# First two attention units of a cross-attention and mixture-of-experts kernel: clears first on GpSimd, the second unit's norms beside the first's, loads in another order

## The chip, the core and the metric

The kernel runs on one core of one Trainium2 chip. The metric is the device time in microseconds (us). The engines are named as in the profile: PE is TensorE (matmuls and transposes) and PEld its weight loads, DVE is VectorE, ACT is ScalarE, POOL is GpSimd, and SP is SyncE, which here only starts DMAs.

## The reference, cut to what matters

```python
def xattn(q, k, v):                      # 8 heads, along the sequence axis of 512
    qn, kn = _l2norm(qh), _l2norm(kh)    # x / max(sqrt(sum(x*x)), 1e-12), 64 values each
    qk = 5.0 * einsum('bhdq,bhdk->bhqk', qn, kn)
    return einsum('bhqk,bhdk->bhdq', softmax(qk), vh)
x = x + xattn(_layernorm(x), ctx_2048, ctx_2048)
x = x + ffn(_layernorm(x))               # 4 experts, top 2 of 4, capacity 512, d 512, hidden 2048
```

x and the context are (4, 512, 512) in float32. The change touches only the first layer norm and the two l2 norms of the attention, of its first two units.

## The kernel before

A unit of attention is 128 rows of x, that is two heads of one batch; there are 16, written as (batch, 0 or 1). For each unit the engines do this:

- DVE takes mean and variance of the x rows (`statistics`, L775 to L781), POOL raises the variance to the power -0.5 (`prepare`, L476, result `rstd`), and DVE writes `x_norm` (`normalize`, L787).
- PE transposes `x_norm` through `bank_m` (`transpose_queries`, L1238) and the context rows through `bank_t` (`values`, L1245). ACT squares both (L617, L625), DVE sums the squares (L794, L804) and floors them (`ss_max`, L797, L807), POOL raises them to -0.5 (`query_norms`, `key_norms`, L476, result `rnorm`).
- DVE widens the queries' factors to 512 columns (`widen_queries`, L836, `wide_q`), PE transposes them back into `bank_m` (`spread_queries`, L1253), and DVE forms the scaled queries as a rounded part and a remainder (`queries`: `q_f` L822, `q_hi` L824, `q_lo` L830).
- ACT rounds the keys (`round_keys`, L642, `k_hi`), POOL takes their remainders (`key_remainders`, L500, `k_lo`). PE then multiplies three terms for the scores (L1266), ACT takes the exponentials (L652), PE the weighted values (L1276) and the sums (L1288).

The order on each engine is written out by hand. `unit(u, behind, ahead)` on each engine works on unit u and on parts of the units beside it: PE begins it with the values and the spread of the next unit, and in its middle transposes the queries of the unit after that. What stands ahead of the first `unit` is a prologue, and the change lies there. In it `bank_m` serves the transposes and the spread of unit (0,0), and then the transposes of (0,1), which wait for `q_hi` of (0,0); `x_norm` is one buffer. POOL also clears `x_got` and `o_got` (L519, L526), 128x2048 each, which are not read before the experts. `cst` is one tile of constants: its first 128 columns are the identity for the transposes, and they come by one DMA (L389), the other 709 columns by a second (L390).

After the attention come the router's choice and then the experts' two matrix products. They are the same in both kernels.

Of the kernel before, what the change touches and what calls it, by code (L numbers as in the profile page):

```python
# [15 lines left out]
ALU = mybir.AluOpType  # L16
ACT = mybir.ActivationFunctionType
# [76 lines left out]
def xattn_moe_kernel(nc, x, ctx_in, Wg, bg, W1, W2, consts, out):  # L94
# [6 lines left out]
    with ExitStack() as stack:  # L101
# [68 lines left out]
        with ExitStack() as phase:  # L170
            def att(name, shape, dt=F32):
                return phase.enter_context(nc.sbuf_tensor(name, shape, dt))
# [3 lines left out]
            c_sq = att("c_sq", [P, D])  # L176
            x_norm = att("x_norm", [P, D])
            x_sq = att("x_sq", [P, D])
# [190 lines left out]
        def _(sp):  # L369
# [16 lines left out]

            load_x((0, 0))
            load_c((0, 0))
            sp.dma_start(ident, consts[:, C_IDENT:C_IDENT + P]).then_inc(ident_in, 16)  # L389
            sp.dma_start(cst[:, C_BEFORE:], consts[:, C_BEFORE:]).then_inc(cst_in, 16)  # L390
            sp.dma_start(wg[:, :, :], Wg.rearrange("(k p) e -> p k e", p=P)).then_inc(wg_in, 16)
            load_x((0, 1))
            load_c((0, 1))
            sp.dma_start(bgb[:, :], bg.rearrange("(a e) -> a e", a=1).broadcast_to([P, E])).then_inc(bg_in, 16)
# [79 lines left out]
        def _(pool):  # L474
# [37 lines left out]
            def finish(u):  # L512
                n = number(u)
                pool.wait_ge(var2_done, n + 1)
                inv_sqrt(rstd2[u[1]][:, :], var2_e[u[1]][:, :], 1).then_inc(rstd2_done, 1)

            prepare((0, 0))
            prepare((0, 1))
            nc.gpsimd.memset(x_got[:, :, :], 0.0).then_inc(got_clear, 1)  # L519
            query_norms((0, 0))  # L520
            key_remainders((0, 0))
            key_norms((0, 0))
            key_remainders((0, 1))
            query_norms((0, 1))
            prepare((1, 0))
            nc.gpsimd.memset(o_got[:, :, :], 0.0).then_inc(got_clear, 1)  # L526

# [82 lines left out]
        def _(act):  # L610
            def square_queries(u, reused):

                n = number(u)
                act.wait_ge(xt_done, n + 1)
                if reused:
                    act.wait_ge(ssq_done, n)
                nc.scalar.activation(x_sq[:, :], bank_m[:, :], ACT.Square).then_inc(xsq_done, 1)  # L617

# [72 lines left out]
            take_v((0, 0), 0)  # L691
            square_queries((0, 1), True)
            round_keys((0, 1), False)
# [76 lines left out]
        def _(dve):  # L770
# [12 lines left out]
            def normalize(u):  # L783

                n = number(u)
                dve.wait_ge(rstd_done, n + 1)
                nc.vector.tensor_scalar(x_norm[:, :], x_all[:, bass.ds(n, 1), :].rearrange("p a d -> p (a d)"),  # L787
                                        mv[u[1]][:, 0:1], rstd[u[1]][:, 0:1], ALU.subtract, ALU.mult).then_inc(xn_done, 1)
# [28 lines left out]
            def queries(u, follow):  # L817


                n = number(u)  # L820
                dve.wait_ge(rq_ready, n + 1)
                nc.vector.scalar_tensor_tensor(q_f[:, :], x_norm[:, :], ALPHA, bank_m[:, :], ALU.mult, ALU.mult  # L822
                                               ).then_inc(q_done, 1)
                nc.vector.scalar_tensor_tensor(q_hi[u[1]][:, :], x_norm[:, :], ALPHA, bank_m[:, :],  # L824
                                               ALU.mult, ALU.mult).then_inc(qhi_done, 1)
                dve.wait_ge(q_done, n + 1)
                dve.wait_ge(qhi_done, n + 1)
                if follow is not None:
                    normalize(follow)
                nc.vector.tensor_tensor(q_lo[u[1]][:, :], q_f[:, :], q_hi[u[1]][:, :].bitcast(F32), ALU.subtract  # L830
                                        ).then_inc(q_split, 1)
# [64 lines left out]
            statistics((0, 1))  # L896
            sum_query_squares((0, 0))
            widen_queries((0, 0))
            sum_key_squares((0, 0))
            queries((0, 0), None)  # L900
            normalize((0, 1))
            dve.wait_ge(cst_in, 16)
# [4 lines left out]
            for n in range(2):  # L907
                nc.vector.tensor_copy(parts[:, :, :, n], cst[:, C_TOK + n * UNITS:C_TOK + (n + 1) * UNITS]
                                      .unsqueeze(1).broadcast_to([P, E, UNITS])).then_inc(bf_done, 1)
            sum_query_squares((0, 1))  # L910
            statistics((1, 0))
            widen_queries((0, 1))

# [319 lines left out]
        def _(pe):  # L1233
            def transpose_queries(u):

                pe.wait_ge(xn_done, number(u) + 1)
                for t in range(TT):
                    last = nc.tensor.transpose(bank_m[:, t * P:(t + 1) * P], x_norm[:, t * P:(t + 1) * P], ident)  # L1238
                last.then_inc(xt_done, 1)
# [68 lines left out]
            pe.wait_ge(ident_in, 16)  # L1308
            pe.wait_ge(cst_in, 16)
            transpose_queries((0, 0))  # L1310
            values((0, 0))
            spread_queries((0, 0))
            pe.wait_ge(qhi_done, 1)
            transpose_queries((0, 1))
            pe.wait_ge(q_split, 1)
            pe.wait_ge(k_split, 1)
            scores((0, 0), 0, False)
            scores((0, 0), 1, False)

            def unit(u, behind, ahead):  # L1320
# [184 lines left out]
```

## Time and profile before

| | us |
|---|---|
| median of 3 runs | 631.37 (631.08 to 632.15) |
| the profiled execution, its own time | 629.77 |
| its span, first to last instruction | 628.0 |
| PE busy | 567.1 (90%) |
| DVE busy | 357.0 (57%) |
| ACT busy | 281.6 (45%) |
| POOL busy | 186.2 (30%) |

A timeline's row gives the start in the span, the busy time, the engine, the line, the operation, the tiles (output<-inputs), the shape and how many instructions are merged, and in brackets how long the engine had been idle and what ended that. Rows of PE overlap, since matmuls are pipelined. A released engine's start is the time at which its last input was there, plus a tenth of a microsecond or so.

### The profile page before, as it was taken

The page shows a single profiled execution, that of the slowest core. Times are in us where ns is not written, and L with a number is a line of the kernel's source. Part 1 is how long each engine was busy: PE and PEld are TensorE (multiplying, and loading weights), DVE is VectorE, ACT ScalarE, POOL GpSimd, SP SyncE. Part 2 cuts the span into 40 slices and gives each one's busy share as a digit, 9 for nine tenths or more (in the row PEclk, how much of TensorE's full clock was granted, in tenths as well). Part 3 has the DMA queues.
Part 4 walks back from the last instruction along what each step waited for, and adds up shares of the span by engine and source line. Part 5 has one row for each costly group of instructions (what it writes and reads, how often), then busy time and mean ns, then how long its engine had stood idle before and what let it go on. Part 6 is the DMA issues. An engine that isn't in the chain of part 4 may idle for free.

```text
span 628.0 us, 8727 instructions
## 1 busy us (share of the span) xinstructions
PE 567.1 (90%) x2842; PEld 407.4 (65%) x2842; DVE 357.0 (57%) x702; ACT 281.6 (45%) x421; POOL 186.2 (30%) x143
## 2 busy tenths in 40 slices
PE   1799999999999512999999999999999999999994
PEld 1445455455454401688888888888888788888883
DVE  4879899899988784534336443354543444424212
ACT  2587776776777240433243333433434324333320
POOL 4556656656642342200030330210420400500002
PEclk9999999999999755699999999999999999999998
DMA  5422332333312113332341543333452332442001
GB/s 144 159 96 85 118 132 89 117 123 95 102 69 94 75 67 103 99 134 68 134 134 68 183 151 134 100 100 110 157 179 88 117 120 97 172 163 68 0 1 67
DMA packets 46600, 67.73 MB, mean 108 GB/s; under 512 B 8560, under 2 KB 25072, under 8 KB 46576
## 3 DMA queue, kind: packets, MB, share of 16 engines
q1 hardware_dynamic: 42736, 54.84, 26.0%
q0 software_dynamic: 3840, 12.59, 6.0%
q8 instruction: 13, 0.21, 0.1%
q14 instruction: 11, 0.09, 0.1%
HBM read 54.70 MB, written 12.64 MB: 107 GB/s over the span
## 4 chain that ended last, share of the span: by engine, by line
PE 64%; DVE 5%; issue 4%; POOL 1%; DMA 1%; POOLq 0%; DVEq 0%; ACT 0%; SPq 0%
PE two L1423 29%; PE four L1453 9%; PE four L1452 9%; PE four L1450 9%; PE two L1276 2%; PE four L1266 2%; DVE junk L1045 1%; PE two L1288 1%; PE bank_t L1304 1%; DMA x_got<-x2n_dram,idx_all 1%; POOL w_lo L532 1%; DMA p_inv<-inv_dram 0%; PE bank_t L1411 0%; PE bank_m L1411 0%; DVE onehot L1132 0%
## 5 line engine op out<-in xcount | busy, mean ns | idle before, releaser
L758 ACT ACTIVATE h_f<-two 128x512 f32<-128x512 f32 x64 | 38.3, 599 | 231.4 <-PE two L1423 231.4
L1206 DVE TENSOR_TENSOR h_lo<-h_f,h_hi 128x512 fp32r<-128x512 f32 x64 | 44.1, 690 | 125.9 <-ACT h_hi L759 125.9
L1423 PE MATMUL two<-xt_hi,w_hi 128*128 (+1 forms) x256 | 102.9, 402 | 0.7 <-ACT xt_hi L747 0.7
L1423 PE MATMUL two<-xt_hi,w_lo 128*128 (+1 forms) x256 | 101.3, 396 | 0.0
L1423 PE MATMUL two<-xt_lo,w_hi 128*128 (+1 forms) x256 | 100.7, 396 | 0.0
L1453 PE MATMUL four<-w_hi,h_lo 128*128 128x512 f32 x256 | 100.5, 393 | 0.0
L1450 PE MATMUL four<-w_hi,h_hi 128*128 128x512 f32 x256 | 100.5, 392 | 0.0
L1452 PE MATMUL four<-w_lo,h_hi 128*128 128x512 f32 x256 | 100.4, 392 | 0.0
L652 ACT ACTIVATE prob<-four,rnorm 128x512 f32<-128x512 f32 x128 | 77.6, 688 | 25.3 <-POOL rnorm L476 18.2
L1176 DVE TENSOR_TENSOR w_lo<-raw,w_hi 128x2048 fp32r<-128x2048 f32 x30 | 68.7, 2291 | 23.3 <-ACT w_hi L685 23.3
L476 POOL TENSOR_TENSOR rnorm<-ss_max,power 128x8 f32<-128x8 f32 x32 | 64.6, 2018 | 49.6 <-DVE ss_max L807 48.3
L605 POOL DMA_INDIRECT out<-o_got,idx_all x16 | 20.2, 1264 | 165.4 <-DVE o_got L1227 163.0
L584 POOL DMA_INDIRECT x_got<-x2n_dram,idx_all x16 | 23.9, 1496 | 140.0 <-DVE idx_all L1163 125.3
L1276 PE MATMUL two<-prob,v_t 128*64 128x512 f32 x256 | 62.0, 605 | 0.0
L685 ACT ACTIVATE w_hi<-raw 128x2048 fp32r<-128x2048 f32 x32 | 61.3, 1918 | 0.0
L1423 PEld LDWEIGHTS two<-xt_hi,w_hi 128*128 128x128 f32 x256 | 48.6, 190 | 11.7 <-ACT xt_hi L747 1.1
L1423 PEld LDWEIGHTS two<-xt_hi,w_lo 128*128 128x128 f32 x256 | 48.6, 190 | 11.1
L1423 PEld LDWEIGHTS two<-xt_lo,w_hi 128*128 128x128 f32 x256 | 48.7, 190 | 10.7
L1453 PEld LDWEIGHTS four<-w_hi,h_lo 128*128 128x128 f32 x256 | 48.1, 188 | 10.8
L1450 PEld LDWEIGHTS four<-w_hi,h_hi 128*128 128x128 f32 x256 | 48.1, 188 | 10.8
L1452 PEld LDWEIGHTS four<-w_lo,h_hi 128*128 128x128 f32 x256 | 48.1, 188 | 10.7
L855 DVE TENSOR_TENSOR half_sum<-prob 128x512 f32<-128x512 f32 x64 | 41.5, 690 | 0.1
(174 smaller groups left out, 741.3 us busy)
## 6 DMA issues: line engine op xcount, KB each, us to landing
raw<-in_L_ffn_W SPq DMA_DIRECT2D x64, 512.0 KB, 4.0
x_all<-in_x SPq DMA_DIRECT2D x16, 256.0 KB, 2.7
c_sb<-in_ctx SPq DMA_DIRECT2D x16, 256.0 KB, 2.8
out<-x_all SPq DMA_DIRECT2D x16, 256.0 KB, 2.0
x2n_dram<-x2n SPq DMA_DIRECT2D x16, 256.0 KB, 2.0
p_inv<-inv_dram SPq DMA_DIRECT2D x30, 128.0 KB, 2.8
few<-p_sum SPq DMA_DIRECT2D x30, 2.0 KB, 2.2
cst<-in_consts SPq DMA_DIRECT2D x1, 354.5 KB, 4.2
```

Of the source, the lines that this page charges most:

```text
L476: return nc.gpsimd.tensor_tensor(dst, src, power[:, 0:n], ALU.pow)
L652: last = nc.scalar.activation(prob[h][t][:, :], s_ps[:, 2 * (t % 2) + h, :], ACT.Exp, scale=rnorm[u[1]][:, 0, t, h:h + 1])
L685: nc.scalar.activation(w_hi[c % SPLIT_BUFS][:, :], raw[c % RAW_BUFS][:, :], ACT.Copy).then_inc(whi_done, 1)
L758: nc.scalar.activation(h_f[m % 2][:, :], z_ps[m % 2][:, :], ACT.Gelu)
L855: nc.vector.tensor_tensor(half_sum[h][n][:, :], prob[h][2 * n][:, :], prob[h][2 * n + 1][:, :], ALU.add).then_inc(halves_done[h], 1)
L1176: nc.vector.tensor_tensor(w_lo[c % SPLIT_BUFS][:, :], raw[c % RAW_BUFS][:, :], w_hi[c % SPLIT_BUFS][:, :].bitcast(F32), ALU.subtract).then ...
L1206: nc.vector.tensor_tensor(h_lo[m % 2][:, :], h_f[m % 2][:, :], h_hi[m % 2][:, :].bitcast(F32), ALU.subtract).then_inc(h_split, 1)
L1276: last = nc.tensor.matmul(o_ps[0][DH * h:DH * (h + 1), :], v_t[u[1]][:, t, h, :], prob[h][t][:, :], start=(t == 0), stop=(t == TT - 1))
L1423: return nc.tensor.matmul(z[:, :], w_part[c][:, w], x_k, start=start, stop=stop)
L1450: nc.tensor.matmul(acc_ps[:, t, :], h_hi[m % 2][:, h], w_hi[c][:, w], start=(m == 0), stop=False)
L1452: nc.tensor.matmul(acc_ps[:, t, :], h_hi[m % 2][:, h], w_lo[c][:, w], start=False, stop=False)
L1453: last = nc.tensor.matmul(acc_ps[:, t, :], h_lo[m % 2][:, h], w_hi[c][:, w], start=False, stop=(m == MT - 1))
```

## The change

SP loads in another order: x of (0,0), the identity, the context of (0,0), x and context of (0,1), and then the other constants and the router's weights. POOL makes both clears at its very start, takes the keys' remainders of (0,0) before the second unit's `rstd` (with a wait for `x_norm`), and raises the query norms of (0,1) ahead of the keys' remainders of (0,1). `x_norm` has two buffers. On PE the transposes of (0,1) go into `two[0]`, which is also `o_ps[0]`, and stand ahead of the spread of (0,0); the wait for the other constants stands behind the first scores. ACT squares the queries of (0,1) from there. DVE normalizes (0,1) and sums its query squares between the steps of (0,0).

```diff
-            x_norm = att("x_norm", [P, D])
+            x_norm = [att(f"x_norm{n}", [P, D]) for n in range(2)]
...
             load_x((0, 0))
+            sp.dma_start(ident, consts[:, C_IDENT:C_IDENT + P]).then_inc(ident_in, 16)
             load_c((0, 0))
-            sp.dma_start(ident, consts[:, C_IDENT:C_IDENT + P]).then_inc(ident_in, 16)
+            load_x((0, 1))
+            load_c((0, 1))
             sp.dma_start(cst[:, C_BEFORE:], consts[:, C_BEFORE:]).then_inc(cst_in, 16)
             sp.dma_start(wg[:, :, :], Wg.rearrange("(k p) e -> p k e", p=P)).then_inc(wg_in, 16)
-            load_x((0, 1))
-            load_c((0, 1))
...
+            nc.gpsimd.memset(x_got[:, :, :], 0.0).then_inc(got_clear, 1)
+            nc.gpsimd.memset(o_got[:, :, :], 0.0).then_inc(got_clear, 1)
             prepare((0, 0))
+            pool.wait_ge(xn_done, 1)
+            key_remainders((0, 0))
             prepare((0, 1))
-            nc.gpsimd.memset(x_got[:, :, :], 0.0).then_inc(got_clear, 1)
             query_norms((0, 0))
-            key_remainders((0, 0))
             key_norms((0, 0))
+            query_norms((0, 1))
             key_remainders((0, 1))
-            query_norms((0, 1))
             prepare((1, 0))
-            nc.gpsimd.memset(o_got[:, :, :], 0.0).then_inc(got_clear, 1)
...
-            square_queries((0, 1), True)
+            square_queries((0, 1), True, o_ps[0])
...
             sum_query_squares((0, 0))
+            normalize((0, 1))
+            sum_key_squares((0, 0))
             widen_queries((0, 0))
-            sum_key_squares((0, 0))
+            sum_query_squares((0, 1))
             queries((0, 0), None)
-            normalize((0, 1))
+            widen_queries((0, 1))
...
-            sum_query_squares((0, 1))
             statistics((1, 0))
-            widen_queries((0, 1))
...
             pe.wait_ge(ident_in, 16)
-            pe.wait_ge(cst_in, 16)
             transpose_queries((0, 0))
             values((0, 0))
+            transpose_queries((0, 1), o_ps[0])
             spread_queries((0, 0))
-            pe.wait_ge(qhi_done, 1)
-            transpose_queries((0, 1))
             pe.wait_ge(q_split, 1)
             pe.wait_ge(k_split, 1)
             scores((0, 0), 0, False)
             scores((0, 0), 1, False)
+            pe.wait_ge(cst_in, 16)
```

POOL, from the start of the program to the remainders of the second unit's keys; `rstd` and `rnorm` carry the number of the unit. Before:

```order
L478 MEMSET power 128x16
L476 ISA
L476 TENSOR_TENSOR rstd0<-var_e0,power 128x1
L476 TENSOR_TENSOR rstd1<-var_e1,power 128x1
L519 MEMSET x_got 128x2048
L476 TENSOR_TENSOR rnorm0<-ss_max,power 128x8
L500 TENSOR_TENSOR k_lo0<-c_sb0,k_hi0 128x512
L476 TENSOR_TENSOR rnorm0<-ss_max,power 128x8
L500 TENSOR_TENSOR k_lo1<-c_sb1,k_hi1 128x512
```

And now:

```order
L478 MEMSET power 128x16
L517 MEMSET x_got 128x2048
L518 MEMSET o_got 128x2048
L476 ISA
L476 TENSOR_TENSOR rstd0<-var_e0,power 128x1
L500 TENSOR_TENSOR k_lo0<-c_sb0,k_hi0 128x512
L476 TENSOR_TENSOR rstd1<-var_e1,power 128x1
L476 TENSOR_TENSOR rnorm0<-ss_max,power 128x8 x2
L476 TENSOR_TENSOR rnorm1<-ss_max,power 128x8
L500 TENSOR_TENSOR k_lo1<-c_sb1,k_hi1 128x512
```

Between the floors and the powers of the first unit's query norms no clear and no remainder stands any more; the ISA row, a reload of the library of instructions that the power comes from, has moved behind the two clears.

DVE, from the sum of the first unit's query squares to its `q_lo`. Before:

```order
L794 TENSOR_REDUCE ss<-x_sq 128x8
L797 TENSOR_SCALAR ss_max<-ss 128x8
L836 COPY wide_q<-rnorm0 128x512
L804 TENSOR_REDUCE ss<-c_sq 128x8
L807 TENSOR_SCALAR ss_max<-ss 128x8
L822 SCALAR_TENSOR_TENSOR q_f<-x_norm,bank_m 128x512
L824 SCALAR_TENSOR_TENSOR q_hi0<-x_norm,bank_m 128x512
L830 TENSOR_TENSOR q_lo0<-q_f,q_hi0 128x512
L787 TENSOR_SCALAR x_norm<-x_all,mv1,rstd1 128x512
```

And now:

```order
L795 TENSOR_REDUCE ss<-x_sq 128x8
L798 TENSOR_SCALAR ss_max<-ss 128x8
L788 TENSOR_SCALAR x_norm1<-x_all,mv1,rstd1 128x512
L805 TENSOR_REDUCE ss<-c_sq 128x8
L808 TENSOR_SCALAR ss_max<-ss 128x8
L837 COPY wide_q<-rnorm0 128x512
L795 TENSOR_REDUCE ss<-x_sq 128x8
L798 TENSOR_SCALAR ss_max<-ss 128x8
L823 SCALAR_TENSOR_TENSOR q_f<-x_norm0,bank_m 128x512
L825 SCALAR_TENSOR_TENSOR q_hi0<-x_norm0,bank_m 128x512
L831 TENSOR_TENSOR q_lo0<-q_f,q_hi0 128x512
L837 COPY wide_q<-rnorm1 128x512
```

The second unit's `x_norm` and query sums have come ahead of the first unit's queries, and its `wide_q` right behind them.

PE, from its first transposes to the first scores. Before:

```order
L1238 MATMUL bank_m<-cst,x_norm 128x128 x4
L1245 MATMUL bank_t<-cst,c_sb0 128x128 x4
L1253 MATMUL bank_m<-cst,wide_q 128x128 x4
L1238 MATMUL bank_m<-cst,x_norm 128x128 x4
L1266 MATMUL four<-q_hi0,k_hi0 128x512 x2
```

And now:

```order
L1239 MATMUL bank_m<-cst,x_norm0 128x128 x4
L1246 MATMUL bank_t<-cst,c_sb0 128x128 x4
L1239 MATMUL two0<-cst,x_norm1 128x128 x4
L1254 MATMUL bank_m<-cst,wide_q 128x128 x4
L1267 MATMUL four<-q_hi0,k_hi0 128x512 x2
```

The second unit's transposes no longer stand between the first unit's spread and its scores.

## Rows read from the trace of the kernel before

**Rows 1.** The page: PE and its granted clock in 40 equal slices.

```profile
PE   1799999999999512999999999999999999999994
PEclk9999999999999755699999999999999999999998
```

**Rows 2.** Busy time in one stretch: length, PE, PEld, DVE, ACT, POOL, granted clock, DMA.

```profile
33.59:43.83 10.24, 10.24 (x63) 4.94 (x61) 7.95 (x19) 8.12 (x14) 5.92 (x5) 1.00 0.19 59
```

**Rows 3.** Timeline of PE, the first 34 us.

```profile
6.45 1.09 PE L1238 MATMUL bank_m<-cst,x_norm 128*128 128x128 f32 x4 [6.45 <-DMA cst<-in_consts]
7.33 1.06 PE L1245 MATMUL bank_t<-cst,c_sb 128*128 128x128 f32 x4
14.03 1.11 PE L1253 MATMUL bank_m<-cst,wide_q 128*128 128x128 f32 x4 [5.64 <-DVE wide_q L836]
17.87 1.09 PE L1238 MATMUL bank_m<-cst,x_norm 128*128 128x128 f32 x4 [2.73 <-DVE x_norm L787]
18.89 0.80 PE L1266 MATMUL four<-q_hi,k_hi 64*128 64x512 f32 x2
...
21.75 0.74 PE L1245 MATMUL bank_t<-cst,c_sb 128*128 128x128 f32 x4
23.80 0.66 PE L1253 MATMUL bank_m<-cst,wide_q 128*128 128x128 f32 x4 [1.31 <-DVE wide_q L836]
...
28.42 0.50 PE L1266 MATMUL four<-q_hi,k_hi 64*128 64x512 f32 x2
```

**Rows 4.** Timeline of DVE, the first 30 us.

```profile
4.41 0.15 DVE L781 TENSOR_SCALAR var_e<-mv 128x1 f32<-128x1 f32 x1
5.33 0.55 DVE L787 TENSOR_SCALAR x_norm<-x_all,mv,rstd 128x512 f32<-128x512 f32 x1 [0.76 <-POOL rstd L476]
7.21 0.69 DVE L775 BATCH_NORM_STATS2 stats<-x_all 128x6 f32<-128x512 f32 x1 [1.34 <-DMA x_all<-in_x]
...
8.23 0.68 DVE L794 TENSOR_REDUCE ss<-x_sq 128x8 f32<-128x512 f32 x1
8.94 1.79 DVE L797 TENSOR_SCALAR ss_max<-ss 128x8 f32<-128x8 f32 x1
12.49 1.48 DVE L836 COPY wide_q<-rnorm 128x512 f32<-128x512 f32 x1 [1.76 <-POOL rnorm L476]
...
14.60 0.17 DVE L807 TENSOR_SCALAR ss_max<-ss 128x8 f32<-128x8 f32 x1
15.18 0.69 DVE L822 SCALAR_TENSOR_TENSOR q_f<-x_norm,bank_m 128x512 f32<-128x512 f32 x1 [0.41 <-PE bank_m L1253]
...
16.58 0.69 DVE L830 TENSOR_TENSOR q_lo<-q_f,q_hi 128x512 fp32r<-128x512 f32 x1
...
23.31 0.43 DVE L836 COPY wide_q<-rnorm 128x512 f32<-128x512 f32 x1 [0.81 <-POOL rnorm L476]
...
26.50 0.69 DVE L830 TENSOR_TENSOR q_lo<-q_f,q_hi 128x512 fp32r<-128x512 f32 x1
```

**Rows 5.** Timeline of POOL, the first 30 us.

```profile
4.72 0.57 POOL L476 TENSOR_TENSOR rstd<-var_e,power 128x1 f32<-128x1 f32 x1 [3.88 <-DVE var_e L781]
...
8.91 1.80 POOL L519 MEMSET x_got<- 128x2048 f32 x1
10.81 1.65 POOL L476 TENSOR_TENSOR rnorm<-ss_max,power 128x8 f32<-128x8 f32 x1
12.43 1.26 POOL L500 TENSOR_TENSOR k_lo<-c_sb,k_hi 128x512 fp32r<-128x512 f32 x1
...
28.07 4.08 POOL L476 TENSOR_TENSOR rnorm<-ss_max,power 128x8 f32<-128x8 f32 x2 [2.51 <-DVE ss_max L807]
```

**Rows 6.** Timeline of SP's queue: the start of the second unit's load of x.

```profile
3.08 0.51 SPq L372 DMA_DIRECT2D x_all<-in_x  x1
```

**Rows 7.** One tile's instructions: shortest, median and longest in ns.

```profile
L855 DVE TENSOR_TENSOR half_sum<-prob x64: 636/691/694, 27.9 to 199.8; 128x512 f32<-128x512 f32 x64
```

**Rows 8.** Busy time in a stretch at the experts' start, columns as in rows 2.

```profile
260.00:265.00 5.00, 5.00 (x21) 4.03 (x20) 1.48 (x2) 3.71 (x5) 0.00 (x0) 0.91 0.02 5
```

More of the change, by code:

```diff
@@ L610, in _, with square_queries @@
         def _(act):
-            def square_queries(u, reused):
+            def square_queries(u, reused, bank=bank_m):
                 n = number(u)
@@ L616, in square_queries @@
                     act.wait_ge(ssq_done, n)
-                nc.scalar.activation(x_sq[:, :], bank_m[:, :], ACT.Square).then_inc(xsq_done, 1)
+                nc.scalar.activation(x_sq[:, :], bank[:, :], ACT.Square).then_inc(xsq_done, 1)
             def square_keys(u, behind):
@@ L786, in normalize @@
                 dve.wait_ge(rstd_done, n + 1)
-                nc.vector.tensor_scalar(x_norm[:, :], x_all[:, bass.ds(n, 1), :].rearrange("p a d -> p (a d)"),
+                nc.vector.tensor_scalar(x_norm[u[1]][:, :], x_all[:, bass.ds(n, 1), :].rearrange("p a d -> p (a d)"),
                                         mv[u[1]][:, 0:1], rstd[u[1]][:, 0:1], ALU.subtract, ALU.mult).then_inc(xn_done, 1)
@@ L821, in queries @@
                 dve.wait_ge(rq_ready, n + 1)
-                nc.vector.scalar_tensor_tensor(q_f[:, :], x_norm[:, :], ALPHA, bank_m[:, :], ALU.mult, ALU.mult
+                nc.vector.scalar_tensor_tensor(q_f[:, :], x_norm[u[1]][:, :], ALPHA, bank_m[:, :], ALU.mult, ALU.mult
                                                ).then_inc(q_done, 1)
-                nc.vector.scalar_tensor_tensor(q_hi[u[1]][:, :], x_norm[:, :], ALPHA, bank_m[:, :],
+                nc.vector.scalar_tensor_tensor(q_hi[u[1]][:, :], x_norm[u[1]][:, :], ALPHA, bank_m[:, :],
                                                ALU.mult, ALU.mult).then_inc(qhi_done, 1)
@@ L1233, in _, with transpose_queries @@
         def _(pe):
-            def transpose_queries(u):
+            def transpose_queries(u, bank=bank_m):
                 pe.wait_ge(xn_done, number(u) + 1)
                 for t in range(TT):
-                    last = nc.tensor.transpose(bank_m[:, t * P:(t + 1) * P], x_norm[:, t * P:(t + 1) * P], ident)
+                    last = nc.tensor.transpose(bank[:, t * P:(t + 1) * P], x_norm[u[1]][:, t * P:(t + 1) * P], ident)
                 last.then_inc(xt_done, 1)
```

## The prediction, as it was made before the changed kernel ran

> **What bounds the kernel now.** I read the page's slices first [rows 1]. PE is busy at nine tenths or more in all but the first slice, slices 14 to 16, and the last, so the end is set by PE's work plus the stretches in which PE has none. One of these is the start: 15.7 us pass before the first slice is over. A stretch of the second unit [rows 2] shows PE busy for 10.24 of 10.24 us while DVE has 7.95, ACT 8.12 and POOL 5.92. From the first unit on, then, the attention runs at PE's pace, and whatever brings PE's first full unit forward brings all that follows forward by as much. The stages behind work on data, not on a clock of their own, and their loads are started by semaphores of the same units. Next I read the timeline of PE [rows 3]: up to 18.89, where the first scores begin, it does 16 transposes in 18.89 us, with idle gaps of 6.45, 5.64 and 2.73 us, and a fourth of 1.31 us at 23.80, behind which there are no more. So the number to follow is the start of the second unit's spread, 23.80. The timelines of DVE and POOL [rows 4, 5] say what each gap waits for.
>
> **The first transposes.** They begin at 6.45, released by the other constants, though `x_norm` is done at 5.33 + 0.55 = 5.88 [rows 3, 4]. The transposes read the identity alone. With the wait moved and the identity second in the queue, they begin 0.06 us behind `x_norm`, as the spread did behind `wide_q` (12.49 + 1.48 = 13.97 to 14.03), so at 5.94: 0.51 us earlier. The clears must be over by then. Each is 1.80 us [rows 5]; from about 0.9 the two end at 4.5, and `rstd` is wanted at 4.72. That covers them by 0.2 us, if the ISA row behind them is short; I take nothing for it, and its upper end is a rival below. The second unit's x, issued as sixth at 3.08 and used at 7.21 [rows 4, 6], is now fourth; with some 830 KB ahead of and in it instead of 1.2 MB I estimate 5.4 from these times, ahead of 5.88, where DVE comes to it. Its statistics were over about 1.0 us behind their start (7.21 to the next sum at 8.23), so now at about 7.0, ahead of the sum of the squares. The first keys' context comes 0.3 us later and is wanted by ACT only for `k_hi`, which POOL needs at 5.9.
>
> **The floor and the clear.** The sum of query squares begins 1.78 us behind the first transposes (8.23 - 6.45), so at 7.72, and `ss_max` 0.71 us later at 8.43. It took 1.79 us before, and the same operation on the keys 0.17 [rows 4]; the long one ended with POOL's clear of `x_got` (8.94 + 1.79 = 10.73 and 8.91 + 1.80 = 10.71) [rows 5]. With no clear there it takes 0.17: 1.62 us saved. It ends at 8.60, and the power runs 8.68 to 10.33 (1.65) [rows 5].
>
> **The widening and the remainders.** `wide_q` took 1.48 us at 12.49 and 0.43 at 23.31; the first lay beside `k_lo` (12.43 + 1.26) [rows 4, 5]. Now `k_lo` runs behind `x_norm` at 5.9 to 7.2, and `rstd` of (0,1) behind it, 7.3 to 7.8, wanted at 8.6. So `wide_q` takes 0.43: 1.05 us saved. The Trainium skill, Advanced Engine Details and Errata, VectorE Performance Modes, says why: the second Vector port is shared, and two-port Vector instructions and GpSimd's block each other. The trace agrees with its 1.79 and 1.48.
> Together 0.51 + 1.62 + 1.05 = 3.18: the first spread moves from 14.03 to 10.85. What is put ahead of it on PE, the transposes of (0,1), needs `x_norm1`, which DVE writes at 8.6 to 9.2; they run 9.3 to 10.4 and are over. On DVE the normalizing (0.55) and the keys' sum and floor (0.68 + 0.17) fill 8.6 to 10.1, under the power's 10.33. Behind the spread DVE sums the second query squares at about 11.0 to 11.9, and the spread's result is there at 10.85 + 1.11 = 11.96. All that costs nothing, though the last by 0.1 us only.
>
> **The first queries and scores.** `q_f` to the end of `q_lo` is 15.18 to 17.27, 2.09 us; now 12.00 to 14.09. Before, the transposes of (0,1) came between `q_lo` and the scores at 18.89; with them gone the scores begin about 0.1 us behind `q_lo`, at 14.2. That is 4.7 us earlier, of which 1.5 is this step.
>
> **The second unit's spread.** The first scores took 21.75 - 18.89 = 2.86 us, then the values; so the values start at 17.06 and the spread could follow. It waited 1.31 us for `wide_q` of (0,1). Now POOL has that unit's factors by about 13.7 (10.33 + 1.65 for the keys' power, then 1.65), takes `k_lo1` to 15.1, and DVE copies by 15.8, all ahead of 17.9. But PE's clock: four transposes took 1.09 to 1.11 us at 6.45, 14.03 and 17.87, 0.74 at 21.75 and 0.66 at 23.80, while the granted clock stands at full there [rows 1]. PE had then worked without a gap for 3.9 us, from 17.87. I put the rise as long behind 14.2, near 18.1, so the values and a part of the spread still run at the lower level of 1.2 GHz: the values take their 0.88 (7.33 - 6.45), and the spread starts at 17.94, 5.86 us earlier; half the spread and the first scores behind it lose 0.35. **Sum: 5.5 us.** The next queries have slack: `q_lo` of (0,1) ended at 26.50 + 0.69 = 27.19, its scores began at 28.42 by PE's order, 1.2 us of cover for DVE's constants' casts and the two statistics, which now stand ahead of them.
>
> **Bounds.** The clock: if it were already up for the first scores, these would gain another 1.2 us; if it rose 2.5 us later, 1.1 would go. It falls and rises once more around the router's choice (slices 14 to 18, and 0.91 in a stretch at the experts' start [rows 8]), and where in the work it rises can move by some 1 us either way. `q_lo1`'s neighbour: `k_lo1` on POOL starts near 13.7, while DVE is at `q_lo` of (0,0), which reads two SBUF tiles. No row shows that pair. The nearest are `half_sum`, which also reads two tiles and kept its 691 ns (636 to 694) [rows 7] beside powers that themselves took 2.04 instead of 1.65 (4.08 for two) [rows 5], and `wide_q`, which was held for all of `k_lo`. So 0 to 1.1 us; I take 0, as `q_lo` is the kind of `half_sum`.
>
> **Rivals.** (A) The ISA row, a reload of a library. Before, it lay in the 3.88 us in which POOL idled ahead of `rstd`, so its cost is between 0 and 3.9, and nothing shows it. Behind the clears at 4.5 it would put `rstd` at up to 8.4 instead of 4.72: 3.7 us of the 5.5 lost, 1.8 left, 629.5. For it: a wait of unknown content. Against: no DMA but the kernel's own is at work in these microseconds.
> The Trainium skill, GPSIMD Engine Reference, Instruction dispatch, says that the first call behind a load of a library pays about 6 us. By that figure the gain would be gone (4.5 + 6 = 10.5, 0.3 slower than now); the 3.88 of the trace leaves no room for it.
> (B) The port between `q_lo` and `k_lo1`, and behind it a late `wide_q` and late statistics: 1.1 us at the scores, and up to 1 more at the second queries, beyond their 1.2 of cover; 3.4 to 4.4 left, 627.5.
> (C) Slower: PE's clock. Its gaps are spread differently, and the rise may come much later than 3.9 us behind 14.2. A microsecond of PE's work at the lower level loses 1 - 0.66/1.10 = 0.4 us. To be 1.3 us slower than before it must cost 6.8 us, so the rise has to come some 17 us late, past 35. It decides from there; 632.7. Against: it has come after 3.9 us of unbroken work, and from 14.2 the work is unbroken.
> (D) The shift does not reach the end, as another engine or a wait further on sets the end of the attention: no change, 631.4. Against: [rows 2].
>
> **How the numbers follow.** The span is 628.0, the execution 629.77 with it, the median of the runs 631.37, 1.6 above. The gain is the same for all: 628.0 - 5.5 = 622.5 for the span, 624.3 for the execution, 625.9 for the median. Forecast 0.73, from 624.2 to 627.0; A 0.09, 626.4 to 629.5; B 0.09, 627.0 to 628.0; C 0.04; D 0.05. The range 624.2 to 628.2 takes in all of B and half of A and leaves out under 2 in 10, the forecast's own tails among them. A measurement of this kernel can tell about 0.2%, 1.3 us, from no change: faster 0.90, same 0.06, slower 0.04.
>
> **What would show it.** In the profile of the changed kernel: first transposes at 5.9, `ss_max` and `wide_q` of (0,0) at 0.17 and 0.43 us, the first scores at 14.2, no idle time of PE between them and the third unit, the second spread near 18.0, and each later unit 5.5 us earlier. `rstd` later than 4.8 is A; `q_lo` longer than 0.75 us or PE idle between the second spread and the second scores is B; transposes of 1.1 us behind 21 is C. I am wrong if these starts are met and the span has not moved with them.

## The result

| | before | changed |
|---|---|---|
| median of 5 runs each | 631.37 us | 624.11 us (622.89 to 624.97) |
| ratio, 95% interval | | 0.9892 (0.9876 to 0.9907) |
| the profiled execution | 629.77 us | 624.58 us |
| its span | 628.0 us | 622.8 us |

The kernel is faster by 1.1%, by 6.8 us if the ratio is put on 631.37 (5.9 to 7.8). The forecast had 5.5. The span it gave, 622.5, was met within 0.3 us. The median it gave, 625.9, is 1.8 too high: 624.11 lies 0.1 below the low end of the range, and 631.37 times the ratio, 624.55, lies 0.35 inside it. Why the span fits and the median doesn't is the main question of the experiments. One execution of one experiment's kernel, 842 us at a granted clock of 0.65, is in none of the numbers below.

The page of the changed kernel, PE and its granted clock in 40 slices, to be held against [rows 1]:

```profile
PE   3999999999998512999999999999999999999994
PEclk9999999999999655799999999999999999999998
```

The first two slices have changed, 3 and 9 tenths instead of 1 and 7. The thirteenth, 8 instead of 9, now ends inside the hole at the router, since the attention is over earlier. The rest is as before. The middle of the attention is too: a stretch of the second unit (length, PE, PEld, DVE, ACT, POOL, granted clock, DMA) shows PE full and the others with the room of [rows 2], and `half_sum` keeps its 0.69 us [rows 7].

```profile
28.68:38.92 10.24, 10.24 (x62) 4.92 (x60) 7.93 (x19) 8.12 (x14) 5.41 (x5) 1.00 0.24 57
L856 DVE TENSOR_TENSOR half_sum<-prob x64: 634/690/694, 22.5 to 195.1; 128x512 f32<-128x512 f32 x64
```

The timeline of PE, for [rows 3]:

```profile
5.97 1.09 PE L1239 MATMUL bank_m<-cst,x_norm 128*128 128x128 f32 x4 [5.97 <-DVE x_norm L788]
9.12 1.11 PE L1239 MATMUL two<-cst,x_norm 128*128 128x128 f32 x4 [1.21 <-DVE x_norm L788]
11.08 1.12 PE L1254 MATMUL bank_m<-cst,wide_q 128*128 128x128 f32 x4 [0.85 <-DVE wide_q L837]
14.38 0.79 PE L1267 MATMUL four<-q_hi,k_hi 64*128 64x512 f32 x2 [2.18 <-DVE q_lo L831]
...
18.15 1.06 PE L1254 MATMUL bank_m<-cst,wide_q 128*128 128x128 f32 x4
19.14 0.80 PE L1267 MATMUL four<-q_hi,k_hi 64*128 64x512 f32 x2
19.73 0.47 PE L1267 MATMUL four<-q_lo,k_hi 64*128 64x512 f32 x2
...
29.18 0.60 PE L1254 MATMUL bank_m<-cst,wide_q 128*128 128x128 f32 x4
```

and the spread of the third unit in the kernel before, which ends the prologue there:

```profile
34.09 0.60 PE L1253 MATMUL bank_m<-cst,wide_q 128*128 128x128 f32 x4
```

PE's four gaps before were 6.45, 5.64, 2.73 and 1.31 us, 16.13 in all. Now there are four others, 5.97, 1.21, 0.85 and 2.18, 10.21 in all, and behind 14.38 PE has none. The second spread comes 23.80 - 18.15 = 5.65 us earlier, the third 34.09 - 29.18 = 4.91, since PE did its first full unit more slowly than before: the pair of score matmuls still takes 0.80 us at 19.14, and 0.47 at 19.73 is the first faster one. From the third spread on the lead hardly moves. It is 4.9 at the first transposes of `key_w` in the router (207.52 to 202.62), 5.0 at the last of them (221.40 to 216.36) and at the experts' start (255.97 to 251.01) and 5.2 at the end of the span.

Timelines of DVE and then POOL, for [rows 4, 5]:

```profile
5.28 0.55 DVE L788 TENSOR_SCALAR x_norm<-x_all,mv,rstd 128x512 f32<-128x512 f32 x1 [0.69 <-POOL rstd L476]
6.41 0.69 DVE L776 BATCH_NORM_STATS2 stats<-x_all 128x6 f32<-128x512 f32 x1 [0.58 <-DMA x_all<-in_x]
...
8.44 0.17 DVE L798 TENSOR_SCALAR ss_max<-ss 128x8 f32<-128x8 f32 x1
...
10.60 0.43 DVE L837 COPY wide_q<-rnorm 128x512 f32<-128x512 f32 x1 [0.74 <-POOL rnorm L476]
...
13.63 0.69 DVE L831 TENSOR_TENSOR q_lo<-q_f,q_hi 128x512 fp32r<-128x512 f32 x1
14.24 1.50 DVE L837 COPY wide_q<-rnorm 128x512 f32<-128x512 f32 x1
```

```profile
2.64 1.80 POOL L518 MEMSET o_got<- 128x2048 f32 x1
4.67 0.57 POOL L476 TENSOR_TENSOR rstd<-var_e,power 128x1 f32<-128x1 f32 x1 [0.22 <-DVE var_e L782]
6.50 1.27 POOL L500 TENSOR_TENSOR k_lo<-c_sb,k_hi 128x512 fp32r<-128x512 f32 x1 [1.26 <-ACT k_hi L643]
...
8.69 5.09 POOL L476 TENSOR_TENSOR rnorm<-ss_max,power 128x8 f32<-128x8 f32 x3 [0.28 <-DVE ss_max L798]
13.76 1.70 POOL L500 TENSOR_TENSOR k_lo<-c_sb,k_hi 128x512 fp32r<-128x512 f32 x1
```

### The profile page after: what moved, and what is told of

It reads as the page before. It is cut to its first block, busy times and chain, and to the rows that moved or that the text cites. A ratio compares the mean times of both kernels' runs of the same rounds, so it can differ in the third digit from the quotient of the medians.

```text
span 622.8 us, 8726 instructions
## 1 busy us (share of the span) xinstructions
PE 568.2 (91%) x2842; PEld 408.5 (66%) x2842; DVE 354.3 (57%) x702; ACT 281.6 (45%) x421; POOL 187.0 (30%) x143
## 4 chain that ended last, share of the span: by engine, by line
PE 65%; DVE 5%; issue 4%; DMA 1%; POOL 1%; POOLq 0%; DVEq 0%; ACT 0%; SPq 0%
PE two L1423 29%; PE four L1453 9%; PE four L1452 9%; PE four L1450 9%; PE two L1277 2%; PE four L1267 2%; DVE junk L1046 1%; PE two L1289 1%; PE bank_t L1305 1%; DMA x_got<-x2n_dram,idx_all 1%; POOL w_lo L533 1%; DMA p_inv<-inv_dram 0%; PE bank_t L1411 0%; PE bank_m L1411 0%; DVE onehot L1133 0%
```

## The experiments

Lines of the changed kernel are one above those of before. No kernel here leaves out any of the computation. In each, "the third spread" is the start on PE of the third unit's spread, 34.09 in the kernel before. Up to it the prologue shows. Behind it each unit of the attention takes 10.2 to 12.0 us, and each takes the same in all traces to 0.04 us, but for three units with a wait for a load, which come up below.

### Before, twice more, and the changed kernel once more

No edit. They ask how typical the two profiled executions are.

> The kernel before itself, for a second trace of it. Its profiled span was 628.0 us, while its other runs have spans of 626.9 to 630.5 us, and the changed kernel's of 621.1 to 623.2, some 6.5 to 7 us less; the two traces show 4.9 us from the third unit to the router, and 5.2 at the end. If runs differ only in when PE's clock rises and falls and in loads landing a little later, a typical trace of before shows the missing 1.5 us in the prologue (third spread later than 34.1) or at the router and the experts' start. If it lies evenly in the attention's units, my account of a pure shift is wrong. Against itself the ratio is 1.000 within 0.2%.

> The kernel before itself for a third trace, if it can be had of a run with a span near its median (628.4 us on this chip). The shift seen between the traces is 4.9 us (first pair) and 5.9 us (second pair) at the third unit, and 5.2 and 5.4 at the end; the medians are 6.8 us apart. A typical trace shows where a further 1 us lies: in the prologue, at the router, or at the experts. Against itself 1.000.

> The changed kernel itself, on the chip of the kernels beside it, to have its distribution of spans next to theirs. The chain gives 4.9 us from the third unit on. If the fall of the median by 7.3 us in the first comparison was more than that (a real cost of the clears or loads later on), the ratio is again 0.989 and the spans differ by about 7 us; if it was the spread of runs, the ratio is 0.991 to 0.992 and the spans differ by 5 us.

Before against itself gave the ratios 0.9998 (0.9984 to 1.0012) and 0.9993 (0.9978 to 1.0008); the changed kernel again 0.9884 (0.9862 to 0.9907), median 623.57. Beside the experiments the kernel before ran 63 times, with a median of 630.4 and spans of 626.9 to 630.5, median 628.6. The changed kernel's nine spans are 621.1 to 623.2, median 621.9 (621.75 for the last four). The medians of the spans are thus 6.7 us apart. DVE's statistics of the second unit, in the kernel before the first and the second time more:

```profile
7.73 0.69 DVE L775 BATCH_NORM_STATS2 stats<-x_all 128x6 f32<-128x512 f32 x1 [1.76 <-DMA x_all<-in_x]
```

```profile
7.89 0.69 DVE L775 BATCH_NORM_STATS2 stats<-x_all 128x6 f32<-128x512 f32 x1 [2.10 <-DMA x_all<-in_x]
```

the third spread in the first of them:

```profile
34.61 0.60 PE L1253 MATMUL bank_m<-cst,wide_q 128*128 128x128 f32 x4
```

and PE in the second, then in the changed kernel again:

```profile
14.71 1.12 PE L1253 MATMUL bank_m<-cst,wide_q 128*128 128x128 f32 x4 [6.27 <-DVE wide_q L836]
...
34.75 0.60 PE L1253 MATMUL bank_m<-cst,wide_q 128*128 128x128 f32 x4
```

```profile
14.24 0.80 PE L1267 MATMUL four<-q_hi,k_hi 64*128 64x512 f32 x2 [2.18 <-DVE q_lo L831]
...
18.96 0.50 PE L1267 MATMUL four<-q_hi,k_hi 64*128 64x512 f32 x2
...
28.68 0.60 PE L1254 MATMUL bank_m<-cst,wide_q 128*128 128x128 f32 x4
```

In the trace that the prediction read, the second unit's x was there at 7.21; in the two others 0.52 and 0.68 us later, and the first spread stands later by as much, at 14.55 and 14.71 instead of 14.03. In the second of them the DMA sets the prologue, because the sum of the first unit's squares queues on DVE behind the second unit's statistics: it begins 2.41 us behind the first transposes instead of 1.78. (In the first of them the constants were 0.52 us late as well.) In the changed kernel x lands at 6.41 and 6.09, ahead of where it is missed. Its second trace also has the third spread 0.5 us earlier, 0.14 of it from the start of the scores and the rest from the clock, which was up at 18.96 instead of about 19.8.

So the lead at the third spread depends on the pair of traces: 4.9 in the first pair, 5.9 and 6.1 for the two others of before against the changed kernel again. But it isn't the whole of the scatter. The trace with 34.61, 0.5 later than 34.09, has the shorter span, 627.3 instead of 628.0. From the experts' first transposes to the last matmul it took 368.2 us and the other 368.9, and over all fourteen traces of this document this stage, whose instructions are the same everywhere, takes 368.0 to 369.6. With three traces of before (middle third spread 34.61) and two of the changed kernel (mean 28.93) the lead is 5.7 us of the 6.7. The last 1.0 us isn't traced to a place: single traces differ by more than that behind the router.

### The clears alone

```diff
+            nc.gpsimd.memset(x_got[:, :, :], 0.0).then_inc(got_clear, 1)
+            nc.gpsimd.memset(o_got[:, :, :], 0.0).then_inc(got_clear, 1)
             prepare((0, 0))
             prepare((0, 1))
-            nc.gpsimd.memset(x_got[:, :, :], 0.0).then_inc(got_clear, 1)
...
             prepare((1, 0))
-            nc.gpsimd.memset(o_got[:, :, :], 0.0).then_inc(got_clear, 1)
```

> The kernel before with one part of the change alone: both clears at POOL's start. My theory, the chain of the prologue: the first floor takes 0.17 us instead of 1.79, everything behind it moves by 1.6 us, the first remainders still lie beside the first wide_q (1.48 us), first scores at 17.3 instead of 18.9, gain 1.6 us (629.8 where before is 631.4). Rival, that the clear of o_got beside the first full unit also cost time, since the median fell by 2 us more than the span of the profiled execution did: gain above 2.5 us.

Ratio 0.998 (0.9964 to 0.9995), that is 1.3 us, and by the medians of the spans, 626.8 beside 628.5, 1.7. The 1.6 expected lies between, and the rival's 2.5 is out. DVE and PE in this kernel:

```profile
9.16 0.17 DVE L797 TENSOR_SCALAR ss_max<-ss 128x8 f32<-128x8 f32 x1
...
11.09 1.48 DVE L836 COPY wide_q<-rnorm 128x512 f32<-128x512 f32 x1 [1.76 <-POOL rnorm L476]
```

```profile
17.48 0.80 PE L1266 MATMUL four<-q_hi,k_hi 64*128 64x512 f32 x2
```

The floor takes 0.17 instead of 1.79, and `wide_q`, whose neighbour `k_lo` has stayed, its old 1.48. The chain from the floor to the scores holds. The third spread is at 32.68.

### The clears put back

The same two lines moved back to their old places in the changed kernel.

> The changed kernel with the two clears in their old places. Chain theory: the first floor takes 1.8 us again, first scores at 16.0 instead of 14.4, 1.6 us later. Since moving the first remainders back moved the first scores by 1.17 us and the third unit by 0.39 us only, PE's clock having risen at the same 19.5 us, I expect the third unit 0.6 to 1.6 us later, 1.1 us slower than the changed kernel. Rival, that the clears have no part in the result once the rest is in: 0.

Ratio 0.9899 (0.9876 to 0.9921), median 624.43 beside 623.57 of the changed kernel; the intervals overlap, so the trace has to tell. DVE, then PE:

```profile
8.52 1.63 DVE L798 TENSOR_SCALAR ss_max<-ss 128x8 f32<-128x8 f32 x1
```

```profile
15.72 0.80 PE L1267 MATMUL four<-q_hi,k_hi 64*128 64x512 f32 x2 [2.18 <-DVE q_lo L831]
...
19.07 0.60 PE L1254 MATMUL bank_m<-cst,wide_q 128*128 128x128 f32 x4
```

The floor is held again, and the scores come 1.34 us later than at 14.38, where 1.6 were expected. But PE is fast at 18.58 already, where the changed kernel was slow until 19.7, and the third spread, at 29.31, is only 0.1 us later (0.6 against the second trace; 0.6 to 1.6 were expected). In this trace the clock gives back most of what the clear takes.

### The first remainders put back

POOL in the changed kernel, in the old order again:

```diff
             prepare((0, 0))
-            pool.wait_ge(xn_done, 1)
-            key_remainders((0, 0))
             prepare((0, 1))
             query_norms((0, 0))
+            key_remainders((0, 0))
```

> The changed kernel with the first keys' remainders back between the two first norms on POOL. Chain theory with the shared port: the first wide_q takes 1.5 us again instead of 0.43, first scores at 15.4 instead of 14.4, 1.0 us slower than the changed kernel. Rival, that it is covered by the slack elsewhere: 0.

Ratio 0.9912 (0.9882 to 0.9943), median 624.97. `wide_q` and the scores:

```profile
10.72 1.49 DVE L836 COPY wide_q<-rnorm 128x512 f32<-128x512 f32 x1 [0.74 <-POOL rnorm L476]
```

```profile
15.55 0.79 PE L1266 MATMUL four<-q_hi,k_hi 64*128 64x512 f32 x2 [2.18 <-DVE q_lo L830]
```

`wide_q` is held for 1.49 us beside `k_lo`, and the scores come 1.17 later. The third spread is at 29.57, 0.4 later than in the changed kernel and 0.9 later than in its second trace. The mechanism is as told; its worth, as with the clears, depends on when the clock rises. The interval overlaps that of the changed kernel, so the 1.0 us expected is neither shown nor ruled out in the time.

### The second unit put back behind the first

PE, DVE and ACT of the changed kernel take the second unit's query steps in the old order:

```diff
-            transpose_queries((0, 1), o_ps[0])
             spread_queries((0, 0))
+            pe.wait_ge(qhi_done, 1)
+            transpose_queries((0, 1))
...
-            normalize((0, 1))
-            sum_key_squares((0, 0))
             widen_queries((0, 0))
-            sum_query_squares((0, 1))
+            sum_key_squares((0, 0))
             queries((0, 0), None)
-            widen_queries((0, 1))
+            normalize((0, 1))
...
+            sum_query_squares((0, 1))
             statistics((1, 0))
+            widen_queries((0, 1))
```

> The changed kernel with one part undone: the second unit's normalizing, transposes, squares and sums stand behind the first unit's queries again, in bank_m (two buffers of x_norm stay). Chain theory: the first spread stays at 11.1, the first scores wait for the four transposes (1.5 us, so 15.9), and the second spread again waits 1.3 us for its factors; second spread at 20.8 instead of 18.15, but then with PE's clock already up, so 2.0 us slower than the changed kernel, 3.0 us faster than before. Rival, that this part only shifts waits about: within 0.7 us of the changed kernel.

Ratio 0.9948 (0.993 to 0.9966), median of the spans 625.3. PE:

```profile
14.54 1.09 PE L1239 MATMUL bank_m<-cst,x_norm 128*128 128x128 f32 x4 [2.73 <-DVE x_norm L788]
...
20.48 0.66 PE L1254 MATMUL bank_m<-cst,wide_q 128*128 128x128 f32 x4 [1.35 <-DVE wide_q L837]
```

Both gaps are back, 2.73 ahead of the transposes and 1.35 ahead of the second spread, as before. The third spread is at 30.76, 1.6 to 2.1 later than in the changed kernel, as expected (2.0). The medians lose more: by the ratios half of the gain is gone, some 3.5 us. What makes up the difference no trace shows. By either measure this part is the largest of the change.

### The loads alone, and the loads put back

The order of SP's loads and the place of PE's wait for the constants, as in the change's diff, on their own in the kernel before; and undone in the changed kernel.

> The kernel before with the loads' part of the change alone: the new order of loads, and PE's wait for all constants moved behind the first scores. By the chain of the trace the first transposes come at 5.9 instead of 6.4 to 7.0, and the sum of squares by as much, so the gain is 0.5 to 1.0 us. The kernel before has runs with spans of up to 630.5 us, which none of its traces shows; if the landing of the constants, which nothing but this wait makes felt, is what lengthens them, the gain in the median is 1.5 us or more and the runs lie closer together.

> The changed kernel with the loads in their old order and the wait for all constants ahead of the first transposes. Chain theory: first transposes at 6.4 instead of 5.97, and the second unit's x, landing at 7.2, puts its statistics and rstd ahead of the first norms on POOL by as much; first scores 0.5 us later, the kernel 0.2 to 0.5 us slower. Rival, that the order of loads carries most of the gain: 1.5 us slower or more.

Alone: ratio 0.9976 (0.9965 to 0.9988), median of the spans 627.1, 1.4 under before. That is more than the 0.5 to 1.0 of the chain and just under the 1.5 of the other view, but the runs, with spans of 625.0 to 628.8, do not lie closer together than those of before. Undone: ratio 0.9894 (0.9868 to 0.9919), median 624.41, 0.8 above the changed kernel's where 0.2 to 0.5 were expected, with intervals that overlap, and with the scores at 14.33 and the third spread at 28.85, so within the changed kernel's own spread. This trace doesn't test the chain: the constants happened to be in time, the first transposes began at 5.92, and x of (0,1) was there at 6.33 though it was issued as sixth. In the five traces with the old order x lands between 6.33 and 7.89, in the nine with the new one it is used between 5.87 and 7.04. At 7.04, in the second trace with 27 fillers (below), the changed order too begins its sum of squares later for it, at 8.06 instead of 7.72.

The profiled execution of the loads alone is the odd one of its kind, with a span of 628.8. Its PE, and then the granted clock in pieces of 2 us (columns as above):

```profile
19.80 0.40 PE L1266 MATMUL four<-q_hi,k_lo 64*128 64x512 f32 x2
22.46 0.66 PE L1253 MATMUL bank_m<-cst,wide_q 128*128 128x128 f32 x4 [1.68 <-DVE wide_q L836]
...
23.58 0.63 PE L1266 MATMUL four<-q_lo,k_hi 64*128 64x512 f32 x2
```

```profile
22.00:24.00 2.00, 1.54 (x8) 1.19 (x10) 1.92 (x7) 0.69 (x2) 2.00 (x2) 0.79 0.97 319
24.00:26.00 2.00, 2.00 (x12) 1.16 (x10) 1.91 (x5) 1.31 (x3) 0.22 (x1) 0.50 1.14 324
26.00:28.00 2.00, 2.00 (x8) 0.42 (x8) 1.81 (x4) 1.22 (x2) 1.27 (x1) 0.86 0.88 301
```

The scores began at 17.54, 1.35 ahead of [rows 3], and PE was fast from 19.4. Then came the gap ahead of the second spread, 1.68 us, and from 23.1 to 26.6 the granted clock stood at 0.50, that is at 1.2 GHz. The third spread came at 34.30, later than before's 34.09. In the kernel before, it follows the second spread by 10.29 us, here by 11.84, so the slow stretch cost 1.55. If it was the gap that brought the clock down, the gap ahead of the second spread, which the change removes, can cost nearly twice its own length; one trace shows it, and nothing was run to test it. A further 0.7 us went much later, where DVE waited 0.95 us for a load at 168.21.

### PE kept busy in the gaps, and in the last gap only

If the slow clock costs the prologue about 2 us, work of no use in PE's gaps should bring it back. Transposes of the identity into an idle bank, 27 in four gaps in the first kernel, nine in the last gap in the other:

```diff
+            def keep_busy(n):
+                for _ in range(n):
+                    nc.tensor.transpose(s_ps[:, 3, 0:P], ident, ident)
...
+            keep_busy(10)
             transpose_queries((0, 0))
             values((0, 0))
+            keep_busy(5)
             transpose_queries((0, 1), o_ps[0])
+            keep_busy(3)
             spread_queries((0, 0))
+            keep_busy(9)
```

> The changed kernel with 27 transposes of the identity into an unused bank, put into PE's gaps of the prologue (10, 5, 3 and 9 of them), so that PE works nearly without a gap from 3.7 us on. It tells what the lower clock costs there, the term that my sum had too small. My theory, that the clock follows PE's work: it rises in the prologue, the first scores take 1.5 us instead of 2.86, four transposes 0.66 instead of 1.1, the second spread comes 1.5 to 3 us earlier, and the kernel is 2.2 us faster than the changed one (1.5 to 3). Rival, that the clock rises at its own time or only with the large matmuls: the first scores stay at 2.86 us, and the kernel is 0 to 0.5 us slower.

> The changed kernel with nine transposes of the identity between the first spread and the first scores only. In the changed kernel the clock rose about 5.4 us behind the first scores, in the kernel with 27 of them before 8 us. If it follows PE's work, the rise comes 1 to 3 us earlier than 19.8, inside the first scores or the second values, and the third unit 0.5 to 1.2 us earlier than in the changed kernel; the median is 0.5 to 1 us lower. If a gap must be filled in all of the prologue for it, the starts are the changed kernel's, and the median too.

> The kernel with PE kept busy in the prologue once more, beside the changed kernel. In its first trace the third unit's spread came 2.45 us earlier than in the changed kernel, but 0.8 us went at a unit where DVE waited for a late load of the sums, and 0.9 us at the router, where the clock fell some microseconds earlier. If these two are chance, the median is 2 us below the changed kernel's. If they are its own (another engine sets the pace, the clock falls at its own time), it is 0 to 1 us below it, and the same two places show in the new trace.

All four gaps: ratios 0.9893 (0.9854 to 0.9933) and, again, 0.9881 (0.9859 to 0.9903), medians 623.6 and 623.29. Last gap only: 0.9896 (0.9881 to 0.9912), 623.87. None differs from the changed kernel's 0.9884, where 2.2 us and 0.5 to 1 us had been expected. PE with nine fillers:

```profile
11.60 2.04 PE L1311 MATMUL four<-cst 128*128 128x128 f32 x9
13.99 0.50 PE L1267 MATMUL four<-q_hi,k_hi 64*128 64x512 f32 x2 [0.35 <-DVE q_lo L831]
...
16.07 0.60 PE L1254 MATMUL bank_m<-cst,wide_q 128*128 128x128 f32 x4
```

The fillers do what they are for: the first scores are fast (0.50 instead of 0.80) and the third spread is at 26.94, 1.7 to 2.2 us earlier than in the changed kernel (26.73 and 27.26 with 27 fillers). The clock thus follows PE's work, and isn't bound to a time of its own or to the large matmuls. But the lead does not get through the router. With nine fillers the last spread is at 177.5 (179.2 in the changed kernel's second trace), the first transposes of `key_w` are at 200.37 beside 202.14, and the last at 215.69 beside 215.65. On the way stands a load, in the kernel with nine fillers and then in the changed kernel again:

```profile
193.25 1.10 SPq L415 DMA_DIRECT2D p_inv<-inv_dram  x2
198.50 0.69 DVE L868 TENSOR_TENSOR o_norm<-o_sb,p_inv 128x512 f32<-128x512 f32 x1 [2.22 <-DMA p_inv<-inv_dram]
```

```profile
195.01 1.09 SPq L415 DMA_DIRECT2D p_inv<-inv_dram  x2
198.43 0.69 DVE L868 TENSOR_TENSOR o_norm<-o_sb,p_inv 128x512 f32<-128x512 f32 x1 [0.40 <-DMA p_inv<-inv_dram]
```

It was issued 1.8 us earlier and was there at the same time, and the whole lead is lost in that wait. With the 27 fillers the same `o_norm` begins at 198.43 and 198.66, no earlier either, behind waits of 1.19 and 1.01 us. Part of their lead is lost before that, in the same way, in both traces; this is the second, and the changed kernel again:

```profile
62.30 1.14 SPq L410 DMA_DIRECT2D few<-p_sum  x2
66.76 0.20 DVE L844 RECIPROCAL few_inv<-few 128x8 f32<-128x8 f32 x1 [1.01 <-DMA few<-p_sum]
```

```profile
63.73 1.14 SPq L410 DMA_DIRECT2D few<-p_sum  x2
67.11 0.19 DVE L844 RECIPROCAL few_inv<-few 128x8 f32<-128x8 f32 x1
```

Again the load was issued 1.4 us earlier and was used only 0.35 earlier, after a wait. The two places named in the last expectation thus show again in the new trace, though at the router it is the wait for the load and not the clock, and the time is 0.3 us below the changed kernel's. The loss is not a single trace's chance. So 4.9 to 6.1 us of a shift passed through the attention, and 2 us more did not. Why these loads then took 4.5 and 5.2 us from issue to use instead of 3.4 isn't shown by any run here; that transfers which other semaphores had started were in their way was not tried, and stays open. A wait of this kind isn't peculiar to the fillers: the trace of the loads alone has one of 0.95 us too. No kernel here beats the changed one.

## Why the prediction was right, and where it was off

- **What bounds the kernel**: right in the main. The lead at the third spread, 4.9, is there at the end as 5.2; rival D had no part. The page's line was read with a slip, since the second slice stood at 7 tenths and not at nine; the timeline that the sum goes by has those gaps. "Whatever brings PE's first full unit forward brings all that follows forward by as much" holds only so far: the fillers' further 2 us were lost in waits for loads.
- **First transposes**: 5.94 forecast, 5.97 in the trace, released by `x_norm`. What I estimated of the loads was off. The second unit's x was there at 6.41, not 5.4, and the remainders began at 6.50 and not at 5.9; both were ahead of their use, so it cost nothing.
- **Floor and clear**: 8.43 forecast, 8.44 in the trace, and 0.17 us long. Right, and shown by two kernels, 1.79 to 0.17 with the clears moved alone and back to 1.63 with them put back. The 1.78 us from the first transposes to the sum held (1.75), with some luck: in the trace read, the squares (8.17) and the second unit's statistics (8.22) were there together, and the prediction counted only the first.
- **Widening and remainders**: 0.43 us, right, and 1.49 with the remainders put back. The first spread came at 11.08 instead of 10.85.
- **Queries and scores**: 14.2 forecast, 14.38 in the trace. Of rival B the first half didn't happen: `q_lo` kept 0.69 beside `k_lo1`, and it was POOL that gave way, 1.70 instead of 1.27. The prediction took 0 for it because of the kind of instruction; here `q_lo` had also begun first, at 13.63, and `k_lo1` at 13.76, so which of the two reasons holds isn't shown. The second half did, since `wide_q` of (0,1) was held for 1.50 us, but it ended at 15.74, 2.4 us ahead of its spread.
- **Second spread**: 17.94 forecast, 18.15 in the trace, without a gap ahead of it: 5.65 us of gain where 5.86 stood.
- **The clock**: the term that was mis-sized in the span. I put the rise 3.9 us behind the first scores and 0.35 us on it. It came 5.4 us behind in the first trace of the changed kernel (14.38 to about 19.8) and 4.7 in the second (14.24 to 18.96). The cost was 5.65 - 4.91 = 0.74 us in the first and 5.79 - 5.41 = 0.38 in the second, where 0.35 stood. The bound, up to 2.5 us later for 1.1, held it.
- **Rival A**, the reload of the library: nothing. The clears end at 2.64 + 1.80 = 4.44 and `rstd` begins at 4.67, 0.09 us behind the end of DVE's `var_e`; in the second trace it begins at 4.53, 0.09 us behind the clears. The Trainium skill, GPSIMD Engine Reference, Instruction dispatch, has about 6 us for the first call of a kernel that has been freshly loaded; nothing of that size shows behind the ISA row here, in the second trace less than 0.1 us.
- **Rival C**: the clock's rise came at 19.8, far from 35.
- **The median**: the step that failed is the last, "the gain is the same for all". The profiled execution of before was 1.6 us under its median, and I took this as an offset that both kernels share. No such shared offset showed. The 63 further executions of before, on two chips, have a median of 630.4, so the 631.37 of five was 1.0 above them, by scatter or by the chip, and the profiled execution 0.6 under them. The changed kernel's profiled execution is not under its median but 0.5 above it (0.8 above that of all nine). The early landing of x at 7.21 can account for up to 0.7 us of before's offset: the kernel before feels it, the changed one, with x there by 6.41, doesn't. Made with the trace where x landed at 7.89, the sum of the forecast would have been 5.5 + 0.7 = 6.2, an estimate, beside 6.7 between the medians of the spans. The rest, as said, has no place. That the forecast came near at all in the median is in part luck: none of its rivals and only one of its bounds, the clock's, pointed to a larger gain, and that one wasn't the cause.

The parts, each by the medians of the runs, hang together but don't add up to exact shares: alone, the clears gave 1.7 and the loads 1.4; taken away, the clears cost 0.9 (624.43 - 623.57), the remainders 1.4, the loads 0.8 and the second unit's order some 3.5 (625.3 - 621.75 in the spans). Alone, the interval of each excludes a ratio of 1. Of those taken away, only the second unit's is clear of the changed kernel's interval. The kernels with the remainders and with the second unit's order put back were measured in another session than the 623.57 and 621.75 they are held against, so these two prices are the rougher ones.

## What to carry to other kernels

Follow a prologue's gain at the start of the first unit that runs without gaps, and look which of the chain's inputs comes by DMA: a profiled execution in which it landed early makes the gain look too small. A clear or a subtraction on POOL that has begun can hold the next copy or scale on DVE until it ends, however small that is, so long clears belong where DVE waits for data anyway. A lead gained at the start counts only until a round trip through DRAM further on has no slack left.

## What the runs showed of the hardware that was not expected

- A DVE instruction of 128x8 elements waited for the end of a 128x2048 clear (1.79 instead of 0.17 us) and a copy of 128x512 for the end of a `k_lo` (1.48 to 1.50 instead of 0.43), while in the pair `q_lo` and `k_lo` it was POOL that took longer. The Trainium skill, Advanced Engine Details and Errata, VectorE Performance Modes, says that the two block each other. In each of these pairs the one that had begun later was the one that waited: the clear began at 8.91 and the floor at 8.94, `k_lo` at 12.43 and `wide_q` at 12.49, and in the changed kernel `q_lo` at 13.63, `k_lo` at 13.76 and `wide_q` at 14.24. No trace here has a `q_lo` that begins behind a `k_lo`. Not all pairs block: a `wide_q` that began at 10.60, while POOL was at its powers, took its 0.43.
- PE's clock rose 5.4 and 4.7 us behind the start of unbroken work in two executions of one kernel. In the kernel before it was 3.9 (17.87 to 21.75), but in its second trace the matmuls were still slow 5.0 us behind (18.39 to 23.38). It was 2.9 in the one with the loads alone (16.53 to 19.4). The Trainium skill, TensorE: Matmul & The Clock Gate, Part 1: The HAM clock gate, says that the number of slow matmuls at the start varies between runs of a kernel, and the traces agree.
- Behind a gap of 1.68 us that ended 3 us after the rise, the clock was down again for 3.5 us in one execution; behind gaps of 1.31, 1.35 and 1.38 us at the same place in other executions it wasn't. Whether the length or the moment decided, or something else, isn't shown.
- The same stage of experts took 368.0 us in one trace and 369.6 in another of the same kernel, the one with 27 fillers. On this kernel one profiled execution can't tell a gain of 1 us.
- The granted clock stood at 1.00 in the records of the prologue (in pieces of 2 us from 10 to 22) while PE's instructions took 1.09 us for what later took 0.66. In this prologue the instructions' own durations tell the clock, and that row doesn't.
